# The values' transposes share the bank of the probabilities' transposes

## The reference

```python
mod = (silu(c) @ wmod)                       # sa, ca, ga, sb, cb, gb; the gates are kept away from 0
h = layernorm(x) * (1 + ca) + sa
q, k, v = h @ wq, h @ wk, h @ wv             # 32 query heads, 8 key/value heads of 128
q, k = rope(q), rope(k)
scores = q @ k.T * 128 ** -0.5               # key j is seen by query i when i - 128 < j <= i
x = x + ga * (softmax(scores) @ v) @ wo
h = layernorm(x) * (1 + cb) + sb
x1, x2 = split(h @ w12.T + b12)
x = x + gb * ((silu(x1) * x2) @ w3.T + b3)
```

## Time and profile before

| | |
|---|---|
| median of 3 runs | 1545.46 us (1545.19 to 1546.64) |
| the profiled execution | 1545.48 us |
| its span | 1543.9 us |
| mean granted clock of TensorE | 0.985 |
| PE busy | 1493.1 us (97%) |
| PE weight loads busy | 1234.7 us (80%) |
| DVE busy | 1112.7 us (72%) |
| ACT busy | 827.7 us (54%) |
| POOL busy | 867.6 us (56%) |

### The profile page before, as it was taken

One profiled execution on the slowest core, in us unless ns is written; L12 is line 12 of the kernel. 1 busy time (PEld: TensorE's weight loads), 2 busy tenths in 40 slices (PEclk: granted clock), 3 DMA queues, 4 the chain that ended last, 5 costly groups with the idle time before them and its releaser, 6 DMA issues.

```text
span 1543.9 us, 26976 instructions
## 1 busy us (share of the span) xinstructions
PE 1493.1 (97%) x7561; PEld 1234.7 (80%) x7561; DVE 1112.7 (72%) x1844; ACT 827.7 (54%) x2195; POOL 867.6 (56%) x892
## 2 busy tenths in 40 slices
PE   6899999999999999988999999999999999988998
PEld 2478888888888888866788888888888888867887
DVE  5677777877777778787787878686868777775432
ACT  3565555556555655555565555565656565554331
POOL 1356565655565656576765656555565656674422
PEclk9999999999999999999999999999999999999999
DMA  8210100101010101022310102020201011120001
GB/s 286 62 49 21 48 20 29 39 28 41 27 41 27 41 27 41 7 75 62 103 42 23 46 0 61 7 61 7 61 7 49 19 48 34 50 90 32 28 28 55
DMA packets 75082, 70.27 MB, mean 46 GB/s; under 512 B 4888, under 2 KB 54048, under 8 KB 75040
## 3 DMA queue, kind: packets, MB, share of 16 engines
q1 hardware_dynamic: 73328, 65.55, 13.7%
q10 hardware_dynamic: 1072, 2.10, 0.4%
q0 software_dynamic: 640, 2.10, 0.4%
HBM read 63.45 MB, written 6.29 MB: 45 GB/s over the span
## 4 chain that ended last, share of the span: by engine, by line
PE 82%; issue 5%; DVE 5%; POOL 4%; ACT 2%; DMA 1%; POOLq 0%; DVEq 0%; ACTq 0%; SPq 0%
PE pP L281 10%; PE pP L283 10%; PE pP L282 10%; PE pOp L281 7%; PE pOp L283 7%; PE pOp L282 7%; PE pS L283 4%; PE pS L282 4%; PE pAv L281 4%; PE pS L281 4%; PE pAv L282 3%; PE pAv L283 3%; PE pTr L291 3%; ACT rA L697 1%; PE pXx L370 1%
## 5 line engine op out<-in xcount | busy, mean ns | idle before, releaser
L1249 POOL TENSOR_SCALAR_AFFINE_SELECT pm<-pT 128x512 fp32r<-128x512 f32 x480 | 390.1, 845 | 475.3 <-DVE pT L874 475.2
L281 PE MATMUL pP<-hT,wp 128*128 128x512 f32 x768 | 312.8, 407 | 2.4 <-ACT rB L646 1.6
L283 PE MATMUL pP<-hT,wp 128*128 128x512 f32 x768 | 301.3, 392 | 0.0
L282 PE MATMUL pP<-hT,wp 128*128 128x512 f32 x768 | 300.2, 391 | 0.0
L1262 POOL TENSOR_TENSOR rB<-rB,tab 128x512 f32<-128x512 f32 x160 | 223.9, 1412 | 33.0 <-ACT rB L646 33.0
L623 ACT CAST oT<-pAv 128x512 fp32r<-128x512 f32 x128 | 74.8, 584 | 301.4 <-PE pAv L283 301.4
L635 ACT ACTIVATE pr<-pS,nb 128x128 f32<-128x128 f32 x512 | 181.5, 372 | 67.7 <-DVE nb L894 67.7
L281 PE MATMUL pOp<-wos,oT 128*128 128x512 f32 x512 | 203.6, 398 | 9.4 <-DVE oT L869 8.1
L904 DVE TENSOR_TENSOR rA<-pP,tab 128x512 f32<-128x512 f32 x160 | 109.9, 688 | 132.3 <-ACT rB L646 132.3
L282 PE MATMUL pOp<-wos,oT 128*128 128x512 f32 x512 | 202.2, 395 | 0.0
L283 PE MATMUL pOp<-wos,oT 128*128 128x512 f32 x512 | 202.0, 395 | 0.0
(11 more groups left out here) (175 smaller groups left out, 3039.3 us busy)
## 6 DMA issues: line engine op xcount, KB each, us to landing
st<-in_L_attn_wq_dram SPq DMA_DIRECT2D x64, 256.0 KB, 3.7
st<-in_L_attn_wo_dram SPq DMA_DIRECT2D x64, 256.0 KB, 2.8
xin<-in_L_attn_x_dram SPq DMA_DIRECT2D x32, 256.0 KB, 3.1
st<-in_L_attn_wk_dram SPq DMA_DIRECT2D x16, 256.0 KB, 2.7
wm<-in_L_wmod_dram SPq DMA_DIRECT2D x4, 1024.0 KB, 8.3
st<-in_L_attn_wv_dram SPq DMA_DIRECT2D x16, 256.0 KB, 2.7
out_dram<-st SPq DMA_DIRECT2D x16, 256.0 KB, 2.0
st<-in_L_ffn_w_dram SPq DMA_DIRECT2D x12, 256.0 KB, 3.1
```

The costliest lines, as they stand in the source:

```text
L281: nc.tensor.matmul(o, hi_l, hi_r, start=start, stop=False, skip_group_check=True)
L282: nc.tensor.matmul(o, hi_l, lo_r, start=False, stop=False, skip_group_check=True)
L283: return nc.tensor.matmul(o, lo_l, hi_r, start=False, stop=stop, skip_group_check=True)
L1249: last = nc.gpsimd.affine_select(out=pm[:, own, part], in_=pT[:, part], compare_op=op, fill=0.0, base=0, pattern=[[0, G], [sign, P]], chan ...
```

## The change

The values' turns inside the attention write to pTr in place of pXx, and `v_hi` and `v_lo` read pTr. The turn ahead of the loop stays with pXx. Two waits of PE are added so that the two kinds of transposes take turns in the bank: ahead of a turn PE waits until `p_lo` of the unit before has read pTr (`u_plo`), and ahead of `trans` in the unit after a turn PE waits until that turn's `v_lo` is done (`j_done`; `v_job` gives the number of the job). Such a unit is one with u % 4 == 0. Nothing is put into pXx in its place.

```diff
--- before.py
+++ after.py
@@ -282,11 +282,13 @@
                 nc.tensor.matmul(o, hi_l, lo_r, start=False, stop=False, skip_group_check=True)
                 return nc.tensor.matmul(o, lo_l, hi_r, start=False, stop=stop, skip_group_check=True)
 
-            def trans(f, u):
+            def trans(f, u, v_before=None):
 
                 f.wait(u_norm, PER_U, u + 1)
                 f.wait(u_phi, PER_U, u)
                 f.wait(u_plo, PER_U, u)
+                if v_before is not None:
+                    f.wait(j_done, PER_J, v_before + 1)
                 for i in range(G):
                     last = nc.tensor.transpose(
                         pTr[:].rearrange("p (h a q) -> p a h q", h=G, a=2)[:, i // 2, 2 * (i % 2):2 * (i % 2) + 2, :],
@@ -362,12 +364,12 @@
                     return PER_R * (NKV - 1) + (10 if before in TURN[:TURN.index(name)] else 5) + SLOT[before] + 1
                 return 0
 
-            def turn_v(f, j):
+            def turn_v(f, j, bank=pTr):
 
                 f.wait(j_act, PER_J, j + 1)
                 f.wait(j_done, PER_J, j - 5)
                 for t in range(CH):
-                    last = nc.tensor.transpose(pXx[:, t * P:(t + 1) * P], rB[:, j % 3, t * P:(t + 1) * P], ident[:])
+                    last = nc.tensor.transpose(bank[:, t * P:(t + 1) * P], rB[:, j % 3, t * P:(t + 1) * P], ident[:])
                 last.then_inc(v_turn, 1)
 
             def ln_transpose(L):
@@ -413,10 +415,21 @@
                             10 * (js + second) + SLOT[name] + 1,
                             PER_R * js + (10 if second else 5) + SLOT[name] - 1 if SLOT[name] >= 2 else None)
 
+            def v_job(u, b):
+
+                if u % CH:
+                    return None
+                if u % NT == CH:
+                    return jbase(b) + PER_J * (u // NT) + SLOT["V"]
+                if u < NT:
+                    return turn_job("V") - PER_J * (b * NKV) if b else None
+                return jbase(b) + 6 + PER_J * (u // NT - 1) + SLOT["V"]
+
             def slot_late(f, u, b):
 
                 js, second = u // NT, u % NT >= CH
                 if u % CH == 3:
+                    f.wait(u_plo, PER_U, u)
                     turn_v(f, jbase(b) + (6 if second else 0) + PER_J * js + SLOT["V"])
 
             def unit_step(f, u, b, jobs, late=lambda: None, prev=True, prev2=True):
@@ -425,7 +438,7 @@
                 if prev2:
                     p_times_v(f, u - 2, b if u >= 2 else b - 1)
                 if prev:
-                    trans(f, u - 1)
+                    trans(f, u - 1, v_job(u, b))
                 jobs()
                 if prev2:
                     out_proj(f, u - 2)
@@ -468,7 +481,7 @@
             for name in SLOT:
                 project(f0, name, 0, 4 + SLOT[name], SLOT[name] + 1, SLOT[name] - 1 if SLOT[name] >= 2 else None)
             mod_row(3)
-            turn_v(f0, 9)
+            turn_v(f0, 9, pXx)
             ln_transpose(4)
             ln_transpose(5)
             mod_row(4)
@@ -539,6 +552,7 @@
                                 filler(4 * (u - 4) + i)
                         if b == 0:
                             if u == 7:
+                                pe.wait_ge(u_plo, PER_U * NKV - 1)
                                 turn_v(Frame(pe, 0), turn_job("V"))
                             for L in TURN_LATE[u]:
                                 ln_transpose(L)
@@ -659,10 +673,10 @@
                 f.wait(j_done, PER_J, j - 2)
                 nc.scalar.copy(rB[:, j % 3, :], pP[j % 2][:]).then_inc(j_act, 1)
 
-            def v_hi(f, ch, v):
+            def v_hi(f, ch, v, bank=pTr):
 
                 f.wait(v_turn, PER_V, v)
-                nc.scalar.copy(kv[:, 0, 1, ch * CT:(ch + 1) * CT], pXx[:]).then_inc(v_half, 1)
+                nc.scalar.copy(kv[:, 0, 1, ch * CT:(ch + 1) * CT], bank[:]).then_inc(v_half, 1)
 
             def jobs_act(f, u, b, js=0):
 
@@ -775,7 +789,7 @@
                     rope_hi(f0, prev_name, 0, j - 1, SLOT[prev_name] + 1)
                 if name == "V":
                     v_copy(f0, j)
-                    v_hi(f0, 0, 1)
+                    v_hi(f0, 0, 1, pXx)
             for L in range(4, 7):
                 ln_act(L)
             act.wait_ge(s_mod, 1)
@@ -920,10 +934,10 @@
                     dst, hi = (blocks(qT[ch], i)[:, :, SLOT[name] - 1, :] for i in (1, 0))
                 nc.vector.tensor_tensor(dst, src, hi, ALU.subtract).then_inc(j_done, 1)
 
-            def v_lo(f, ch, v):
+            def v_lo(f, ch, v, bank=pTr):
 
                 f.wait(v_half, PER_V, v)
-                nc.vector.tensor_tensor(kv[:, 1, 1, ch * CT:(ch + 1) * CT], pXx[:],
+                nc.vector.tensor_tensor(kv[:, 1, 1, ch * CT:(ch + 1) * CT], bank[:],
                                         kv[:, 0, 1, ch * CT:(ch + 1) * CT], ALU.subtract).then_inc(j_done, 1)
 
             def add_y(f, u, b):
@@ -1092,7 +1106,7 @@
                 if i in (1, 2):
                     ln_stats(3 + i)
             rope_lo(f0, "Q3", 0, 8, 5)
-            v_lo(f0, 0, 1)
+            v_lo(f0, 0, 1, pXx)
             ln_stats(6), ln_lo(4), ln_apply(6), ln_stats(7), gate_row(1), ln_lo(5), ln_apply(7), ln_lo(6), ln_lo(7)
             nc.vector.tensor_copy(sel[:], ident[0:B, 0:B].unsqueeze(2).to_broadcast([B, B, P])).then_inc(s_gdve, 1)
 
```

## The result

The changed kernel takes 1565.83 us (median of 4 runs, 1564.25 to 1566.44), beside 1545.33 us for the kernel before (4 runs): ratio 1.0131, 95% interval 1.0113 to 1.0148. It is slower by 20.5 us. The forecast was 1572.6 us, with a range from 1567.5 to 1587.

What follows compares the result with a forecast made beforehand. PE was taken to bound the loop, with no idle time. Lateness of 23.47 us over 14 stalls plus 3.64 us restart gave 27.1 us on 1545.48, so 1572.6 us; 8-in-10 range 1567.5 to 1587.

Steps and rivals of the forecast that it cites:

- Which waits bind, and which don't: PE's `trans` waits for `v_lo` at 14 first turns; second turns, batch change and last head of batch 0 cost 0.
- Lateness 1.69 us, unchanged by the stall: Steady first turns: `v_lo` ends 1.69 us after PE is ready for `trans`; 13 × 1.69 = 21.97 us, head 0 adds 1.50.
- No other engine hands the delay on: Behind the stalled `trans`: `p_hi` moves to about 191.3, still before ACT's exponentials and DVE's `p_lo`, so no second delay.
- No cost of the bank, of the wait for `p_lo`, of waits that are met: At the turns: other bank address costs nothing, `p_lo` wait and its register addition 0, second-turn waits met 1.23 us early.
- Restart 0.26 us: PE's pick-up after each stalled `trans`: 0.26 us, between 0.10 and 0.42; 14 × 0.26 = 3.64 us (1.4 to 5.9).
- The estimate from the Trainium skill: Exposed weight load as the whole restart at `trans`: 14 × 0.107 = 1.5 us, a total 2.1 us lower than forecast.
- PE has no idle time in which something added could vanish: Steady loop: PE busy 80.95 of 81 us, so a stall of PE goes into the total in full.
- The range's low end: Low end of the 8-in-10 range for the whole kernel: 1567.5 us, the deficits without restart.
- less than all: Rival: one or two loop stalls swallowed and no restart, 21.97 us or a little less, 1567.5 us; chance 0.05.
- The clock: Rival: PE's clock falls in stalls, 1.6 us each; half of them 1584 us, all 1595; chance 0.18.
- Not slower: Rival: `v_lo` ends within 3.17 us of the turn in DVE's queue, all stalls 0, 1545.5 us; chance 0.05 with variants.

Runs made afterwards that it cites:

- the shorter mask: The kernel before, without one of the four selections of POOL's mask of unit 4: 1541.84 us (5 runs), ratio 0.9962.

## Why the prediction was wrong, and where it was right

- *Which waits bind, and which don't:* right. 14 stalls that count, those of rows 3, 5 and 7; none at the second turns, the change of batch or the last head of batch 1; and the 2.19 us of rows 8 disappear in the idle time that was there. The clock fell behind that stall, but behind the hole of before too, and the stretch became 0.46 us shorter, not longer.
- *Lateness 1.69 us, unchanged by the stall:* right. `v_lo` ends 4.86 us after the turn in both kernels. Moving it by one place moves the cost by 0.59 × 14.
- *No other engine hands the delay on:* right, but narrowly. `p_hi` now ends at 192.88 and ACT's exponentials start at 192.94, 6.34 us after the turn as before.
- *No cost of the bank, of the wait for `p_lo`, of waits that are met:* right, by the two kernels with the waits and the own bank.
- *Restart 0.26 us:* too large. At the stalled `trans` PE starts 0.06 after `v_lo` ends and the next group comes 0.41 later instead of 0.35: 0.12 in all. I took the middle between rows of other places. The reason I had, that the wait for `v_lo` is the last before `trans`, may be why PE starts so soon. In the loop the start comes 0.06 us after the other engine's end with no wait behind, 0.13 with one (the mask), and 0.22 with two (`out_proj`). But in the last head of batch 0, which is unrolled, `trans` starts 0.15 after `v_lo` (687.46 to 687.61), and no run isolates this, so the cause stays open. The 0.20 of the transposes at 671.16 was measured against the wrong group: a group that layer norms' transposes follow, as they do there, takes 0.44 without a wait (674.90 to 675.34, in the kernel before), so 0.11 of its 0.55 was restart. The term was 3.64 us and is 14 × 0.12 = 1.7: 2.0 us too much. The estimate from the Trainium skill (TensorE: Matmul & The Clock Gate, LDWEIGHTS), 107 ns for each restart, was nearer in size to the 0.12 us measured. Half of those lie ahead of the start, though, and no run shows that an exposed weight load is what they are.
- *"PE has no idle time in which something added could vanish":* this step failed. I read it from 80.95 us busy of 81. The busy time is a union of bars, each of which reaches 0.16 us beyond the start of the next (0.39 us drawn, 0.23 apart; 0.27 drawn, 0.11 apart), so a wait of 0.2 us is all but hidden in such a row. By the heads' lengths with the shorter mask, the wait for POOL's mask cost PE 0.27 us in every regular head of batch 0 and 0.19 in batch 1. The stall makes PE late enough that the mask is always ready. A stall's 1.81 us (1.69 + 0.12) thus cost 1.54 in heads 1 to 6 of batch 0 and 1.62 in batch 1. In head 0 of batch 0 it cost 1.22 for 1.60 at the place. Together 3.3 us too much, and with the restart 5.3 of the 6.9 us between the 27.1 of the sum and the 20.2 of the spans.
- *The rest,* 1.65 us, is the parts outside the heads with stalls (−0.38, −0.46, −0.81). Parts like these differ by more than that between the profiles of this case; I don't give them a cause. They are about as large as the 1.7 us by which the time lies below the range, so the two terms above alone would have put it close to the range's low end.
- *The range's low end* was the lateness without restart. It lacked the case that came true: a small wait further on that a stall covers. My rival "less than all" went as far as 1567.5 and no farther.
- *The clock:* right for this change (the granted clock of the head shown is 1.00, and all regular heads with a stall are equally long), and the reason, that 1.6 us is nearer to the 1.60 that held than to the 2.19 that fell, stands. But idle time of one length doesn't decide it: at 2.17 to 2.19 us 8 of 13 held, and one of 1.98 fell.
- *"Not slower":* its decisive point, `v_lo` within 3.17 us of the turn, is confirmed by the kernel that puts `v_lo` first, and the splits ahead of it were the reason, as said.

## What to carry to other kernels

Before two uses share a buffer, look at how soon the *last* reader of the first use is served in its own engine's queue, not only at how long it takes: here 0.7 us of work came 3 us late because an order written by hand had put it last, and moving it ahead of the splits made the shared buffer free and gained 4 us besides. Whether an engine with pipelined instructions is ever waiting is read from the distance between starts, against the usual distance for that shape, and not from its busy share. A new stall costs less than its length when the engine had small waits downstream, and a reordering that removes one of them can hand it to the next input (here from POOL's mask to DVE's low part) with no change of the time.

## What the runs showed of the hardware

A wait of PE that is already met, with a register addition in front of it, costs nothing measurable (46 waits a run, 42 of them with the addition: ratio 1.0005, 0.9995 to 1.0014). A wait for `v_lo` that isn't met restarts the transposes 0.06 us after DVE's instruction ends, in the loop, and costs 0.06 more behind it; in the unrolled last head they start 0.15 after it. Idle times of PE in the loop's dense work cost the clock in no case of 14 at 1.39 to 1.59 us, in 6 of 14 at 1.98 to 2.19 us, and in 10 of 14 at 2.56 to 2.79 us, 1.6 us each.
